# A two-layer gated cross-attention block on one core: start-up loads, key/value units ahead of attention, and one tile moved ahead of a LayerNorm

## The chip, the cores and the metric

The kernel runs on one core of a Trainium2 chip. A core has five engines, each with its own queue of instructions carried out in order: PE (TensorE, matrix products and transposes), DVE (VectorE), ACT (ScalarE), POOL (GpSimd) and SP (SyncE, which here issues the DMAs). They meet only at semaphores. The metric is the time of one execution on the device, in microseconds (us).

## The reference, cut to what matters

```
x = x + tanh(g_xattn[0]) * experts(layernorm(x), token_ids, ctx)       # stage 1: ctx is keys and values of four experts
x = x + tanh(g_ffn[0])   * bitnet_ffn(layernorm(x), Wgate, Wup, Wdown) # stage 2: 8-bit tokens, ternary weights, Hadamard
x = x + tanh(g_xattn[1]) * attention(layernorm(x), ctx, Wq, Wk, Wv, Wo) # stage 3: 16 heads of 128, softmax
x = x + tanh(g_ffn[1])   * moe(layernorm(x))                            # stage 4: 32 small experts, top 8, and a shared one
```

x and ctx are 1024 tokens of 256 values. Experts: `silu(h @ Wg.T) * (h @ Wu.T) @ Wd.T` with Wg, Wu and Wd all equal to the expert's 256 rows of ctx; each token takes one expert. Attention needs keys `K = ctx @ Wk` and values `V = ctx @ Wv`, which depend on the input ctx and the weights alone.

## The kernel before

All products are float32, made of three products of rounded parts (high times low, low times high, high times high; lines 1557 to 1559). So every operand is split into a high part (made by ACT with a copy that rounds) and a low part (a subtraction on DVE or POOL).

The tokens are two groups (g = 0, 1) of four tiles of 128. PE's program is written out by hand: the expert scores (12 products of 512 columns per expert and group), the expert outputs (12 products for each of eight tiles, `y0` to `y7`), then a pipeline over eight tiles of the feed-forward part. Its stages are named by letters: Q (transposes of the quantised tokens), G and U (gate and up products), F (transposes of the inner values), H (Hadamard products), C (transposes of the quantised values), D (down products), N (transposes of the next LayerNorm), P (queries). After that 32 steps of attention, one per head and group, and at last stage 4.

Keys and values are made in 64 **units**. One unit is six products of 512 columns into one PSUM bank, an eviction by ACT, and one or two stores to HBM, from which attention reads them back. Four units share one 512 KB block of weights, which is loaded, split by ACT (`block_high`) and POOL (`block_low`), and lies in one of two slots. The table FILLS says where PE's program has units ahead of attention: before, 26 of them (`s0` and `s1` are at the very start, `y6` is behind tile 6 of the expert outputs, `u0` behind the up product of tile 0, and so on). The other 38 lie in the steps of attention, one or none in each half step (`m0`, `e0`, ...). PE waits before unit k until ACT has evicted unit k-2 (`kv_taken`), since the units ahead of attention use two banks in turn.

POOL's order in the feed-forward part: for each tile the four butterfly additions of the Hadamard step (`fly`, lines 632 to 638) once DVE has multiplied gate and up (`inner`, line 1362); behind tile 0 the low part of block 4, `block_low(4)`. DVE's order: additions of the expert outputs to x (line 1200), LayerNorm of group 0 and its quantisation, then group 1 likewise. `qtok` are quantised tokens, `am` the largest magnitude of each token.

## Time and profile before

| | us |
|---|---|
| median of three runs (lowest, highest) | 568.3 (567.09, 570.09) |
| the profiled execution, its own time | 568.33 |
| its span in the trace | 566.5 |
| PE busy | 537.0 (95%) |
| DVE busy | 389.8 (69%) |
| ACT busy | 350.9 (62%) |
| POOL busy | 320.5 (57%) |

The time of an execution has 1.8 us more than the span, in which the trace shows no instruction. PE's instructions overlap, so that the ends of its rows are modelled; the distance from start to start tells what one takes. The column for PE's clock tells what the throttle granted. "idle before" is how long an engine did nothing before an instruction, with the engine that ended it.

### The profile page before, as it was taken

Reading aid. Unit: us, or ns where it says so; the run is one execution under the profiler, and the core shown is the slowest. Engines: PE = TensorE matmul, PEld = TensorE weight load, DVE = VectorE, ACT = ScalarE, POOL = GpSimd, SP = SyncE. Lnnn points to the kernel's source line nnn. Section 1 sums busy time; section 2 is a strip of 40 time slices with the busy share of each in tenths; the row PEclk is TensorE's granted clock in tenths of the full one; section 3 lists DMA queues with packets and bytes.
Section 4 is the critical chain, followed back from the end, with each engine's and each line's share of the span. In section 5 each row is a group of like instructions: output and inputs, shape, how many; then the busy total and the mean of one; then the engine's idle time right before and its main releaser. Section 6 shows DMA issues by size and latency. Waiting matters only on the chain.

```text
span 566.5 us, 9626 instructions
## 1 busy us (share of the span) xinstructions
PE 537.0 (95%) x3240; PEld 462.2 (82%) x3240; DVE 389.8 (69%) x822; ACT 350.9 (62%) x723; POOL 320.5 (57%) x320
## 2 busy tenths in 40 slices
PE   3999998998999999999999999999999989999997
PEld 3877766777778988999999999989998878777786
DVE  4867988689956575656655576646665757878883
ACT  3651155666478676766757565745757665777882
POOL 2579137999348797655544424426698465762220
PEclk9999999999999999999999999989999998999999
DMA  8901136510057768677696768534354735356651
GB/s 278 357 23 46 47 111 185 189 38 1 20 185 226 222 186 261 218 247 224 217 289 191 244 206 229 188 98 163 115 189 149 241 125 174 112 146 189 217 178 39
DMA packets 66672, 95.78 MB, mean 169 GB/s; under 512 B 6336, under 2 KB 38848, under 8 KB 66624
## 3 DMA queue, kind: packets, MB, share of 16 engines
q1 hardware_dynamic: 66624, 95.17, 53.0%
q8 instruction: 27, 0.44, 0.3%
q14 instruction: 21, 0.17, 0.1%
HBM read 67.23 MB, written 27.92 MB: 168 GB/s over the span
## 4 chain that ended last, share of the span: by engine, by line
PE 69%; DVE 11%; POOL 6%; ACT 5%; issue 4%; DMA 3%; SPq 1%; DVEq 0%; POOLq 0%
PE ps L1557 20%; PE ps L1558 19%; PE ps L1559 19%; PE ps L1662 4%; PE ps L1767 2%; PE ps L1751 2%; DMA k_hl<-k_scratch 1%; DVE e_r L1472 1%; PE ps L1774 1%; DMA blk_raw<-in_w_blocks 1%; DVE qtok L1223 1%; ACT q2T L921 1%; PE ps L1780 1%; DMA cw_row<-cw_scratch 1%; DVE e_lo L1482 1%
## 5 line engine op out<-in xcount | busy, mean ns | idle before, releaser
L657 POOL TENSOR_TENSOR probs<-probs,rsum 128x512 f32<-128x512 f32 x64 | 66.4, 1041 | 60.5 <-DVE rsum L1252 60.4
L1247 DVE TENSOR_REDUCE nmax<-ps 128x2 f32<-128x512 f32 x64 | 44.0, 688 | 35.6 <-PE ps L1559 35.3
L959 ACT ACTIVATE probs<-ps,nmax 128x256 f32<-128x256 f32 x128 | 59.7, 481 | 1.6 <-DVE nmax L1247 1.4
L578 POOL TENSOR_TENSOR kv_w_lo<-blk_raw,kv_w_hi 128x1024 fp32r<-128x1024 f32 x16 | 38.9, 2431 | 37.2 <-ACT kv_w_hi L826 37.2
L1045 ACT ACTIVATE e_hi<-e_r 128x512 fp32r<-128x512 f32 x64 | 40.2, 629 | 30.4 <-DVE e_r L1472 29.6
L1472 DVE SCALAR_TENSOR_TENSOR e_r<-ps,cw_row 128x512 f32<-128x512 f32 x64 | 43.6, 684 | 12.8 <-PE ps L1559 10.3
L1238 DVE TENSOR_TENSOR pT_lo<-ps,pT_hi 128x512 fp32r<-128x512 f32 x64 | 43.7, 685 | 11.9 <-ACT pT_hi L965 11.4
L780 POOL TENSOR_TENSOR e_lo<-e_sq,e_hi 128x512 fp32r<-128x512 f32 x19 | 24.5, 1292 | 45.1 <-ACT e_sq L1051 42.6
L1243 DVE TENSOR_TENSOR oT_lo<-ps,oT_hi 128x512 fp32r<-128x512 f32 x32 | 22.1, 691 | 40.2 <-ACT oT_hi L969 40.2
L965 ACT ACTIVATE pT_hi<-ps 128x512 fp32r<-128x512 f32 x64 | 38.3, 600 | 15.9 <-PE ps L1662 15.8
L969 ACT ACTIVATE oT_hi<-ps 128x512 fp32r<-128x512 f32 x32 | 19.1, 597 | 40.8 <-PE ps L1559 40.8
L584 POOL TENSOR_TENSOR k_hl<-k_hl 128x512 fp32r<-128x512 f32 x18 | 23.8, 1322 | 32.1 <-ACT k_hl L894 32.1
L1662 PE MATMUL ps<-eye,probs 128*128 128x128 f32 x256 | 39.0, 275 | 1.6 <-DVE kv_out L1278 1.0
L837 ACT ACTIVATE kv_hi<-ps 128x512 fp32r<-128x512 f32 x38 | 22.9, 602 | 26.9 <-PE ps L1559 26.9
L1557 PE MATMUL ps<-pT_hi,v_hl 128*128 128x256 f32 x128 | 36.6, 286 | 1.1 <-DVE pT_lo L1238 0.5
L1557 PE MATMUL ps<-k_hl,qT_lo 128*128 128x256 f32 x128 | 37.3, 292 | 0.0
L1559 PE MATMUL ps<-k_hl,qT_hi 128*128 128x256 f32 x128 | 36.4, 285 | 0.0
L1558 PE MATMUL ps<-k_hl,qT_hi 128*128 128x256 f32 x128 | 36.3, 284 | 0.0
L1559 PE MATMUL ps<-wo_hi,oT_hi 128*128 128x256 f32 x128 | 36.2, 283 | 0.0
L1558 PE MATMUL ps<-wo_lo,oT_hi 128*128 128x256 f32 x128 | 36.2, 283 | 0.0
L1557 PE MATMUL ps<-wo_hi,oT_lo 128*128 128x256 f32 x128 | 36.2, 283 | 0.0
L1559 PE MATMUL ps<-pT_hi,v_hl 128*128 128x256 f32 x128 | 36.2, 282 | 0.0
(299 smaller groups left out, 1876.9 us busy)
## 6 DMA issues: line engine op xcount, KB each, us to landing
cw_row<-cw_scratch SPq DMA_DIRECT2D x64, 256.0 KB, 3.6
v_hl<-v_scratch SPq DMA_DIRECT2D x24, 512.0 KB, 3.6
blk_raw<-in_w_blocks SPq DMA_DIRECT2D x23, 512.0 KB, 4.4
k_scratch<-kv_out SPq DMA_DIRECT2D x32, 256.0 KB, 2.6
v_scratch<-kv_out SPq DMA_DIRECT2D x32, 256.0 KB, 3.2
k_hl<-k_scratch SPq DMA_DIRECT2D x14, 512.0 KB, 3.5
v_scratch<-kv_hi SPq DMA_DIRECT2D x24, 256.0 KB, 2.8
blk_raw<-in_w_tail SPq DMA_DIRECT2D x10, 512.0 KB, 4.6
```

Source lines behind the costliest of these rows:

```text
L578: nc.gpsimd.tensor_tensor(lo[:, :], blk_raw[j % 2][:, :], hi[:, :].bitcast(F32), ALU.subtract).then_inc(blk_done, 1)
L657: nc.gpsimd.tensor_tensor(probs[:, b, :, :], probs[:, b, :, :], rsum[:, b, :].unsqueeze(2).to_broadcast([P, 2, S]), ALU.mult).then_inc(pro ...
L959: last = nc.scalar.activation(probs[:, b, t, :], ps[:, S_BANK[b], t * S:(t + 1) * S], ACT.Exp, bias=nmax[:, b, t:t + 1], accum_out=esum[:, ...
L965: nc.scalar.activation(pT_hi[:, b, :, :].rearrange("p k q -> p (k q)"), ps[:, P_BANK[b], :], ACT.Copy).then_inc(p_hi_done, 1)
L1045: nc.scalar.activation(e_hi[i % 4][:, :], e_r[i % 2][:, :], ACT.Square).then_inc(e_hi_done, 1)
L1238: V.tensor_tensor(pT_lo[:, b, :, :].rearrange("p k q -> p (k q)"), ps[:, P_BANK[b], :], pT_hi[:, b, :, :].rearrange("p k q -> p (k q)").bi ...
L1247: V.tensor_reduce(nmax[:, b, :], ps[:, S_BANK[b], :].rearrange("p (t k) -> p t k", t=2), AX.X, ALU.max, negate=True).then_inc(max_done, 1)
L1472: V.scalar_tensor_tensor(e_r[i % 2][:, :], ps[:, UP_BANK[i % 4], :], 0.0, cw_row[i % 4][:, :], ALU.max, ALU.mult).then_inc(root_done, 1)
L1557: mm(dst, l_lo, r_hi, start=first, stop=False, **kw)
L1558: mm(dst, l_hi, r_lo, start=False, stop=False, **kw)
L1559: return mm(dst, l_hi, r_hi, start=False, stop=last, **kw)
L1662: last = nc.tensor.transpose(ps[:, P_BANK[b], k * S + t * P:k * S + (t + 1) * P], probs[:, b, t, k * P:(k + 1) * P], ident)
```

## The change

It has these parts:

- **Start.** The first block of key weights and the first half of ctx are loaded in four pieces (128, 256, 256 and 384 KB) and split in as many. Until they come PE does ten products of zeros that nothing reads. The four units of `s0` (before three) do their products as high-high, low-high, high-low, so that each waits only for what it needs. The two units of `s1` (before one) do four of their six products ahead of the transposes of the first LayerNorm and the other two behind them. Their context is split on DVE right behind the first LayerNorm.
- **POOL's start.** The token masks are made in halves and later; `block_low(1)` comes before the rounding of the ternary weights, not before the third of them. On ACT `block_high(1)` comes ahead of the first silu.
- **Expert outputs.** The first tile of outputs is added to x ahead of the low part of z of group 1. Q of group 0 transposes in two halves, each waiting for one bank.
- **Tile 0 of the feed-forward part.** DVE multiplies its inner values ahead of the LayerNorm of group 1. Those of tile 1 come ahead of the quantisation of group 1. The rounding of that quantisation goes from DVE to ACT (`second_tokens`), between the first and the second eviction of `u1`.
- **Units.** 28 of the 64 units lie ahead of attention: one more each in `s0`, `s1` and `d4` (behind D of tile 4), one less in `d6`. All later units are numbered two further, and the blocks follow in another order.

```diff
-        BLOCKS = [("K", 0), ("V", 0), ("K", 1), ("V", 1), ("K", 2), ("Q", 0), ("K", 3), ("O", 0), ("V", 2), ("Q", 1), ("V", 3),
-                  ("O", 1), ("V", 0), ("Q", 2), ("K", 1), ("O", 2), ("V", 1), ("Q", 3), ("K", 2), ("V", 2), ("O", 3),
+        BLOCKS = [("K", 0), ("V", 0), ("K", 1), ("V", 1), ("K", 2), ("Q", 0), ("K", 3), ("V", 2), ("O", 0), ("Q", 1), ("V", 3),
+                  ("V", 0), ("O", 1), ("K", 1), ("Q", 2), ("O", 2), ("V", 1), ("K", 2), ("Q", 3), ("V", 2), ("O", 3),
...
-        FILLS = {"s0": 3, "s1": 1, "a11": 1, "y2": 1, "y6": 4, "u0": 2, "g1": 1, "u1": 3, "f0": 3, "g2": 1, "f1": 2, "d4": 0, "d5": 1, "c6": 1, "d6": 2}
+        FILLS = {"s0": 4, "s1": 2, "a11": 1, "y2": 1, "y6": 4, "u0": 2, "g1": 1, "u1": 3, "f0": 3, "g2": 1, "f1": 2, "d4": 1, "d5": 1, "c6": 1, "d6": 1}
...
+            sp.dma_start(blk_raw[0][:, 0:D], w_blocks[0, 0, :, 0:D]).then_inc(ld_keys[0], 16)
+            for c in range(DC):
+                sp.dma_start(cT_raw[:, c, 0:GT], ctx_t[c * P:(c + 1) * P, 0:GT]).then_inc(ld_ctx[c], 16)
+            sp.dma_start(blk_raw[0][:, D:4 * D], w_blocks[0, 0, :, D:4 * D]).then_inc(ld_keys[1], 16)
             sp.dma_start(xr[:, 0:GN, :], x[0:GT, :].rearrange("(n p) d -> p n d", p=P)).then_inc(ld_x[0], 16)
             sp.dma_start(eye[:, :], ident_in).then_inc(ld_const, 16)
-            load_context(1)
+            sp.dma_start(cT_raw[:, :, GT:T], ctx_t[:, GT:T].rearrange("(c p) n -> p c n", p=P)).then_inc(ld_ctx[2], 16)
...
+                for k in FILL_AT["s0"][2 * i:2 * i + 2]:
+                    store_unit(k)
...
-                pool.wait_ge(blk_hi_done, j + 1)
+                pool.wait_ge(blk_hi_done, j)
...
-            pool.wait_ge(blk_hi_done, 1)
             for n in range(4):
                 s = slice(n * D, (n + 1) * D)
+                pool.wait_ge(first_keys_hi_done, 1 if n == 0 else 2)
                 nc.gpsimd.tensor_tensor(kv_w_lo[0][:, s], blk_raw[0][:, s], kv_w_hi[0][:, s].bitcast(F32), ALU.subtract)\
                     .then_inc(first_keys_done if n < 3 else blk_done, 1)
             pool.wait_ge(ld_ids, 32)
-            for e in range(1, NB):
-                nc.gpsimd.tensor_scalar(ge_row[:, e - 1, :], ids_row[:, :], float(e * TOK_PER_EXPERT), None, ALU.is_ge)\
-                    .then_inc(masks_ready, 1)
+            for g in range(NG):
+                s = slice(g * GT, (g + 1) * GT)
+                if g:
+                    pool.wait_ge(h_ready, NG)
+                else:
+                    pool.wait_ge(ctx_late_done, DC)
+                for e in range(1, NB):
+                    nc.gpsimd.tensor_scalar(ge_row[:, e - 1, s], ids_row[:, s], float(e * TOK_PER_EXPERT), None, ALU.is_ge)\
+                        .then_inc(masks_ready, 1)
+            block_low(1)
             for i in range(3):
-                if i == 2:
-                    block_low(1)
...
-            pool.wait_ge(scales_ready, 1)
             block_low(2)
             block_low(3)
...
-                elif n == 7:
-                    key_low(1)
 
             pool.wait_ge(h_ready, NG + 1)
             block_low(7)
+            key_low(1)
             block_low(8)
             block_low(9)
...
+            act.wait_ge(ld_keys[0], 16)
+            nc.scalar.activation(kv_w_hi[0][:, 0:D], blk_raw[0][:, 0:D], ACT.Copy).then_inc(first_keys_hi_done, 1)
+            for c in range(DC):
+                act.wait_ge(ld_ctx[c], 16)
+                context_high(c, 0)
+            act.wait_ge(ld_keys[1], 16)
+            nc.scalar.activation(kv_w_hi[0][:, D:4 * D], blk_raw[0][:, D:4 * D], ACT.Copy).then_inc(first_keys_hi_done, 1)
+            for k in FILL_AT["s0"]:
+                if k == 2:
+                    act.wait_ge(ld_ctx[2], 16)
+                    for c in range(DC):
+                        context_high(c, 1)
+                take_unit(k)
...
+            block_high(1)
             for g in range(NG):
                 if g:
                     first_expert(g)
                     take("a11")
-                    block_high(1)
                 act.wait_ge(a_taken, (NB - 1) * (g + 1))
                 nc.scalar.activation(a_silu[:, :, :], a_sel[:, g, :, :], ACT.Silu).then_inc(a_silu_done, 1)
                 act.wait_ge(z_ready, g + 1)
                 nc.scalar.activation(z_hi[:, g, :, :], a_sel[:, g, :, :], ACT.Copy).then_inc(z_hi_done, 1)
             take("y2")
+            block_high(2)
             take("y6")
-            block_high(2)
+            block_high(3)
...
+            def second_tokens():
+
+                take_unit(FILL_AT["u1"][0])
+                act.wait_ge(q1_scaled, 1)
+                act.wait_ge(q1T_filled, 1)
+                for n in range(GN, NT):
+                    last = nc.scalar.activation(qtok[:, n - GN, :], h[:, n, :], ACT.Copy, scale=am_r[:, n:n + 1], bias=ROUND)
+                last.then_inc(q1_rounded, 1)
+                for k in FILL_AT["u1"][1:]:
+                    take_unit(k)
...
-                    take("u" + str(i))
-                if i < 2:
-                    block_high(3 + i)
+                    if i == 1:
+                        second_tokens()
+                    else:
+                        take("u" + str(i))
+                if i == 1:
+                    block_high(4)
...
+                    take("d4")
...
+            V.memset(zeros.bitcast(F32), 0.0).then_inc(zeros_ready, 1)
+            for c in range(DC):
+                dve.wait_ge(ctx_hi_done, c + 1)
+                V.tensor_tensor(cT_lo[:, c, 0:GT], cT_raw[:, c, 0:GT], cT_hi[:, c, 0:GT].bitcast(F32), ALU.subtract).then_inc(ctx_done, 1)
             dve.wait_ge(ld_x[0], 16)
             norm(0).then_inc(h_ready, 1)
+            for c in range(DC):
+                dve.wait_ge(ctx_hi_done, DC + c + 1)
+                V.tensor_tensor(cT_lo[:, c, GT:T], cT_raw[:, c, GT:T], cT_hi[:, c, GT:T].bitcast(F32), ALU.subtract).then_inc(ctx_late_done, 1)
...
-            context_low(1)
...
+                V.tensor_tensor(a_sel[:, g, :, :], a_sel[:, g, :, :], a_silu[:, :, :], ALU.mult).then_inc(z_ready, 1)
+                if g:
+                    add_experts([0])
+                dve.wait_ge(z_hi_done, g + 1)
+                V.tensor_tensor(z_lo[:, g, :, :], a_sel[:, g, :, :], z_hi[:, g, :, :].bitcast(F32), ALU.subtract).then_inc(z_done, 1)
...
+            def token_scales(g):
 
                 s = slice(g * GN, (g + 1) * GN)
                 own(V.tensor_reduce(am[:, s], h[:, s, :], AX.X, ALU.max, apply_absolute_value=True))
-                own(V.tensor_scalar(am[:, s], am[:, s], Q_EPS, None, ALU.max))
-                own(V.reciprocal(am_r[:, s], am[:, s]))
-                own(V.tensor_scalar(am_r[:, s], am_r[:, s], 128.0, None, ALU.mult))
+                own(V.tensor_scalar(am_c[:, s], am[:, s], Q_EPS, 1.0 / 128.0, ALU.max, ALU.mult))
+                return V.reciprocal(am_r[:, s], am_c[:, s])
+
+            def quantise(g):
+
+                s = slice(g * GN, (g + 1) * GN)
                 if g:
-                    dve.wait_ge(q1T_filled, g)
-                for n in range(GN):
-                    last = V.tensor_scalar(qtok[:, n, :], h[:, g * GN + n, :], am_r[:, g * GN + n:g * GN + n + 1], ROUND,
-                                           ALU.mult, ALU.add)
-                own(last)
+                    dve.wait_ge(q1_rounded, 1)
+                else:
+                    own(token_scales(0))
+                    for n in range(GN):
+                        last = V.tensor_scalar(qtok[:, n, :], h[:, n, :], am_r[:, n:n + 1], ROUND, ALU.mult, ALU.add)
+                    own(last)
...
+            inner_values(0)
             dve.wait_ge(y0_taken, NT)
             own(norm(1, 2))
             for i in range(NT + 3):
                 if i == NT + 2:
                     query_low(0)
                     query_low(1)
-                if i < NT:
-
-                    b = pair_of["U", i]
-                    dve.wait_ge(silu_done, i + 1)
-                    dve.wait_ge(up_values_filled, i + 1)
-                    V.tensor_tensor(inner[:, i % 2, :], inner[:, i % 2, :], ps[:, b:b + 2, :].rearrange("p a n -> p (a n)"),
-                                    ALU.mult).then_inc(inner_done, 1)
-                if i == 0:
+                if 0 < i < NT:
+                    inner_values(i)
+                if i == 1:
+                    token_scales(1).then_inc(q1_scaled, 1)
                     quantise(1)
...
+            def first_keys_begin(k):
+
+                kind, quad, n, g, j = UNITS[k]
+                tokens = slice(g * GT, (g + 1) * GT)
+                pe.wait_ge(first_keys_hi_done, 1 if n == 0 else 2)
+                for c in range(DC):
+                    pe.wait_ge(ctx_hi_done, g * DC + c + 1)
+                    mm(ps[:, fill_bank(k), :], kv_w_hi[0][:, (n * DC + c) * P:(n * DC + c + 1) * P], cT_hi[:, c, tokens],
+                       start=(c == 0), stop=False)
+                if n == 3:
+                    pe.wait_ge(blk_done, 1)
+                else:
+                    pe.wait_ge(first_keys_done, n + 1)
+                for c in range(DC):
+                    mm(ps[:, fill_bank(k), :], kv_w_lo[0][:, (n * DC + c) * P:(n * DC + c + 1) * P], cT_hi[:, c, tokens],
+                       start=False, stop=False)
+
+            def first_keys_end(k):
+
+                kind, quad, n, g, j = UNITS[k]
+                for c in range(DC):
+                    pe.wait_ge(ctx_late_done if g else ctx_done, c + 1)
+                    last = mm(ps[:, fill_bank(k), :], kv_w_hi[0][:, (n * DC + c) * P:(n * DC + c + 1) * P],
+                              cT_lo[:, c, g * GT:(g + 1) * GT], start=False, stop=(c == DC - 1))
+                last.then_inc(kv_filled, 1)
...
+                    if k < 2 * GN:
+                        first_keys_begin(k)
+                        first_keys_end(k)
+                        continue
...
-                    for c in range(DC):
+                    chunks = range(DC) if n else [fill_bank(k) - b for k in FILL_AT["y6"][-2:]]
+                    for c in chunks:
+                        if n == 0:
+                            pe.wait_ge(kv_taken, FILL_AT["y6"][-2:][chunks.index(c)] + 1)
...
+            pe.wait_ge(zeros_ready, 1)
+            for _ in range(10):
+                mm(ps[:, 7, :], zeros[:, 0:P], zeros, start=True, stop=True)
             fill_units("s0")
+            for k in fills("s1"):
+                pe.wait_ge(kv_taken, k - 1)
+                first_keys_begin(k)
             pe.wait_ge(ld_const, 16)
             transpose_norm(0, 0, 6)
-            fill_units("s1")
+            for k in fills("s1"):
+                first_keys_end(k)
```

How the order moves on PE at the start: the last unit of `s0`, the transposes of the first LayerNorm (`ps<-eye,h`) and `s1`. Before:

```order
L1557 MATMUL ps<-cT_hi,kv_w_lo0 128x512
L1558 MATMUL ps<-cT_lo,kv_w_hi0 128x512
L1559 MATMUL ps<-cT_hi,kv_w_hi0 128x512
L1571 MATMUL ps<-eye,h 128x128 x8
L1557 MATMUL ps<-cT_hi,kv_w_lo0 128x512
L1558 MATMUL ps<-cT_lo,kv_w_hi0 128x512
L1559 MATMUL ps<-cT_hi,kv_w_hi0 128x512
L1557 MATMUL ps<-cT_hi,kv_w_lo0 128x512
L1558 MATMUL ps<-cT_lo,kv_w_hi0 128x512
L1559 MATMUL ps<-cT_hi,kv_w_hi0 128x512
L1557 MATMUL ps<-hT_hi,cT_lo 128x512
```

With the change:

```order
L1640 MATMUL ps<-cT_hi,kv_w_lo0 128x512 x2
L1648 MATMUL ps<-cT_lo,kv_w_hi0 128x512 x2
L1633 MATMUL ps<-cT_hi,kv_w_hi0 128x512 x2
L1640 MATMUL ps<-cT_hi,kv_w_lo0 128x512 x2
L1633 MATMUL ps<-cT_hi,kv_w_hi0 128x512 x2
L1640 MATMUL ps<-cT_hi,kv_w_lo0 128x512 x2
L1621 MATMUL ps<-eye,h 128x128 x8
L1648 MATMUL ps<-cT_lo,kv_w_hi0 128x512 x4
L1607 MATMUL ps<-hT_hi,cT_lo 128x512
L1608 MATMUL ps<-hT_lo,cT_hi 128x512
L1609 MATMUL ps<-hT_hi,cT_hi 128x512
```

The transposes now stand behind four whole units and the first eight products of two more, whose last four products follow them.

How it moves on ACT, from the silu of tile 1 (`inner<-ps,c_gate`) on. Before:

```order
L910 ACTIVATE inner<-ps,c_gate 128x1024
L835 ACTIVATE kv_out<-ps 128x512 x4
L826 ACTIVATE kv_w_hi<-blk_raw 128x1024
L925 ACTIVATE fT_hi<-ps 128x1024
L835 ACTIVATE kv_out<-ps 128x512 x3
L910 ACTIVATE inner<-ps,c_gate 128x1024
```

With the change:

```order
L947 ACTIVATE inner<-ps,c_gate 128x1024
L846 ACTIVATE kv_out<-ps 128x512 x2
L923 ACTIVATE qtok<-h,am_r 128x256 x4
L846 ACTIVATE kv_out<-ps 128x512 x2
L838 ACTIVATE kv_w_hi<-blk_raw 128x1024
L965 ACTIVATE fT_hi<-ps 128x1024
L846 ACTIVATE kv_out<-ps 128x512 x3
L947 ACTIVATE inner<-ps,c_gate 128x1024
```

Four steps that write `qtok` now stand between two pairs of evictions, and `kv_w_hi` of block 4 behind them.

How it moves on DVE, between the last expert outputs (`xr<-ps,tgm,xr`) and the LayerNorm of group 1. Before:

```order
L1200 SCALAR_TENSOR_TENSOR xr<-ps,tgm,xr 128x256 x3
L1083 BN_STATS st<-xr 128x6 x2
L1088 BN_AGGR mv<-st 128x2 x4
L1091 TENSOR_SCALAR ln_v<-mv 128x4
L1094 TENSOR_SCALAR ln_i<-ln_v 128x4
```

With the change:

```order
L1219 SCALAR_TENSOR_TENSOR xr<-ps,tgm,xr 128x256 x3
L1281 TENSOR_TENSOR inner<-inner,ps 128x1024
L1124 BN_STATS st<-xr 128x6 x2
L1129 BN_AGGR mv<-st 128x2 x4
L1132 TENSOR_SCALAR ln_v<-mv 128x4
```

The multiplication of the inner values of tile 0 now stands ahead of the statistics.

## Rows read from the trace of the kernel before

**Rows 1.** Busy time by stretch: us, each engine (instructions), PE clock share, DMA share, GB/s.

```profile
0.00:163.00 163.00, 144.85 (x793) 114.15 (x794) 126.97 (x286) 81.03 (x97) 98.69 (x74) 1.00 0.37 121
163.00:420.00 257.00, 254.71 (x1720) 232.86 (x1720) 160.65 (x337) 172.76 (x442) 149.12 (x151) 0.99 0.66 207
```

**Rows 2.** The longest wait of PE up to 163 us: in total, times, longest.

```profile
PE ps L1557 <- POOL kv_w_lo L595: 8.7, 1, 8.7
```

**Rows 3.** Timeline of the start: us, duration, engine, line, operation [idle before].

```profile
12.27 0.63 PE L1559 MATMUL ps<-cT_hi,kv_w_hi 128*128 128x512 f32 x1
12.69 0.63 PE L1557 MATMUL ps<-cT_hi,kv_w_lo 128*128 128x512 f32 x1
12.88 2.10 DVE L1113 TENSOR_SCALAR h<-xr,mv,ln_y 128x256 f32<-128x256 f32 x4
13.13 8.67 POOL L599 TENSOR_SCALAR ge_row<-ids_row 128x1024 int32<-128x1024 int32 x3 [2.49 <-DMA ids_col<-in_ids]
14.41 0.39 PE L1557 MATMUL ps<-cT_hi,kv_w_lo 128*128 128x512 f32 x1
14.64 0.39 PE L1558 MATMUL ps<-cT_lo,kv_w_hi 128*128 128x512 f32 x1
16.42 0.69 DVE L1143 TENSOR_TENSOR hT_lo<-ps,hT_hi 128x512 fp32r<-128x512 f32 x1 [0.78 <-ACT hT_hi L848]
17.95 1.22 DVE L1133 TENSOR_TENSOR cT_lo<-cT_raw,cT_hi 128x1024 fp32r<-128x1024 f32 x1
18.11 0.47 PE L1557 MATMUL ps<-hT_hi,cT_lo 128*128 128x512 f32 x1
```

**Rows 4.** Timeline of the expert choice, ACT and DVE.

```profile
32.86 2.10 DVE L1186 TENSOR_TENSOR a_sel<-a_sel,a_silu 128x1024 f32<-128x1024 f32 x1 [1.06 <-ACT a_silu L877]
35.96 1.01 ACT L859 ACTIVATE a_sel<-ps 128x1024 f32<-128x1024 f32 x1
37.45 0.60 ACT L835 ACTIVATE kv_out<-ps 128x512 f32<-128x512 f32 x1 [0.47 <-PE ps L1559]
```

**Rows 5.** Timeline, the two waits of PE in the expert outputs.

```profile
53.87 0.50 PE L1557 MATMUL ps<-cT_hi,z_lo 128*128 128x512 f32 x1 [1.07 <-DVE xr L1200]
71.48 1.09 PE L1742 MATMUL ps<-eye,qtok 128*128 128x128 f32 x8 [0.69 <-ACT kv_out L835]
```

**Rows 6.** Timeline of the first tiles of the feed-forward part, and a contended step at 143 us.

```profile
77.69 0.75 DVE L1083 BATCH_NORM_STATS2 st<-xr 128x6 f32<-128x256 f32 x2
79.10 0.17 DVE L1094 TENSOR_SCALAR ln_i<-ln_v 128x4 int32<-128x4 int32 x1
82.70 1.22 DVE L1362 TENSOR_TENSOR inner<-inner,ps 128x1024 f32<-128x1024 f32 x1
83.83 1.21 DVE L1216 TENSOR_REDUCE am<-h 128x4 f32<-128x1024 f32 x1
84.87 1.29 POOL L632 TENSOR_TENSOR fly<-inner 128x512 f32<-128x512 f32 x1
89.99 2.44 POOL L578 TENSOR_TENSOR kv_w_lo<-blk_raw,kv_w_hi 128x1024 fp32r<-128x1024 f32 x1
90.17 1.06 PE L1757 MATMUL ps<-eye,inner 128*128 128x128 f32 x8 [2.12 <-POOL inner L638]
100.52 1.06 PE L1757 MATMUL ps<-eye,inner 128*128 128x128 f32 x8 [0.20 <-POOL inner L638]
143.12 1.27 POOL L584 TENSOR_TENSOR k_hl<-k_hl 128x512 fp32r<-128x512 f32 x1
143.22 1.20 DVE L1094 TENSOR_SCALAR ln_i<-ln_v 128x4 int32<-128x4 int32 x1
```

**Rows 7.** Timeline of the last tiles of the feed-forward part.

```profile
140.84 0.47 DVE L1388 SCALAR_TENSOR_TENSOR xr<-ps,am,xr 128x256 f32<-128x256 f32 x1
141.02 0.47 PE L1767 MATMUL ps<-had,fT_lo 128*128 128x256 f32 x2 [1.17 <-issue]
148.52 0.47 PE L1767 MATMUL ps<-had,fT_lo 128*128 128x256 f32 x2 [1.02 <-ACT q L931]
```

More of the change, by code:

```diff
@@ L106, in flamingo_two_layer_kernel @@
         head_weights(1, early)
+        zeros = wq_hi[1][:, 0:512]
         region = ExitStack()
@@ L839, in _, with context_high @@
-            for g in range(NG):
-                s = slice(g * GT, (g + 1) * GT)
-                act.wait_ge(ld_ctx[g], 16)
-                nc.scalar.activation(cT_hi[:, :, s], cT_raw[:, :, s], ACT.Copy).then_inc(ctx_hi_done, 1)
-                if g == 0:
-                    block_high(0)
-            take("s0")
+                    take_unit(k)
+            def context_high(c, g):
+                nc.scalar.activation(cT_hi[:, c, g * GT:(g + 1) * GT], cT_raw[:, c, g * GT:(g + 1) * GT], ACT.Copy).then_inc(ctx_hi_done, 1)
```

131 lines of the change are left out of this document (63 added, 68 removed).

## The prediction, made before the changed kernel was run

> **What bounds the kernel now.** I read busy time by stretch first, to see where PE leaves time unused. From 163 to 420 us, the attention steps, PE is busy 254.7 of 257 us: there only less work for PE brings time. Up to 163 us it is busy 144.9, so 18 us are idle [rows 1]. The waits of PE say who ends them: 8.7 us are the start, until the first low parts of the keys are there [rows 2]; the rest is waits of about 1 to 2 us, which I looked up one by one in the timeline [rows 5 to 7]. Work that the change moves out of attention is worth its full length if it fits into such idle time, and nothing otherwise.
>
> One unit is six products of 512 columns. They start 0.43 us apart at 12.27 and 12.69 us, and 0.23 apart at 14.41 and 14.64 [rows 3], so a unit costs 6 x 0.233 = 1.4 us there, and 2.6 at the slow spacing. By columns over spacing these are the clock levels of 1.2 and 2.4 GHz; PE had issued products back to back for 4.4 us (8.7 to 13.1) before the faster one. The column for the granted clock reads 1.00 for the whole part up to 163 us [rows 1] and doesn't show this; the spacing does.
>
> **The change part by part.** Times are those of the profiled execution, 568.33 us (span 566.5 and 1.8 around it); the median of the three runs is 568.3, so the sum stands for it too.
>
> *Start: two more units.* Whether they are free depends on when the expert products run without a wait, at 18.11 us before [rows 3]. That is set by DVE, which makes the low parts of the transposes (the first at 16.42) just before. DVE's last step of the LayerNorm (12.88 to 14.98) takes 2.10 us beside POOL's masks; the masks now come later, and without them I expect 0.7 us less, 14.3. But 1.22 us of context splitting, which lay behind at 17.95, now stand ahead of the low parts. DVE was idle for 0.78 us there, waiting for ACT, and the splitting fills that [rows 3]: 18.1 - 0.7 + 1.2 - 0.8 = 17.8, and with a gap between five steps instead of four 18.1 again. PE's side has room: with loads in pieces real products can start by about 6 us (estimate: 1 MB came by 6.7, when ACT began on the last of it in the chain), four units at 1.4 take it to 11.9 and eight products to 13.8, ahead of the transposes at about 14.3. Even at the slow spacing until 10 us it gets there by 14.5, so the zeros matter little. Two units fewer remain in attention, where PE is full: -2 x 1.4 = **-2.8**. Bounds: -4.2 (free at 16.7) and 0 (free at 20.9).
>
> *ACT ahead of the first silu.* `block_high(1)` is a pass over 1024 columns, about 1.0 us like the copy at 35.96 [rows 4]. Behind it in ACT's queue stand silu, z and the copy of the first expert of group 1, which PE needs for its third expert. That copy ended at 36.97, and PE's unit before the third expert ended at about 37.4 (ACT took it at 37.45): 0.4 us of slack. 1.05 - 0.4 = **+0.7**. Bounds: 0, as the multiplication (2.10 us at 32.86, held by POOL) may now find a gap, and +1.7, if it is held for one more pass of POOL.
>
> *Expert outputs.* The wait of 1.07 at 53.87 is for the first tile's addition, which now uses DVE's idle time while ACT makes z: **-1.1** (-1.1 to 0). Q's wait of 0.69 at 71.48 [rows 5] is for the last bank; half of the transposes (0.45 us) now goes into it: **-0.4** (-0.7 to 0). The wait before `u0` stays, since that is PE's own last tile and its additions behind it.
>
> *First tiles of the feed-forward part.* This is the part that decides. Before, PE waits 2.12 us at 90.17 for tile 0's butterfly on POOL, and that waits for `inner` at 82.70, which stood behind the LayerNorm begun at 77.69. Now `inner` is first: 77.7 to 78.9, and POOL's four additions of 1.29 us run from 79.0 to 84.2. That wait is gone. What is late next: the LayerNorm now runs beside POOL. At 143.22 `ln_i`, 0.17 us when alone at 79.10, took 1.20, as long as POOL's addition at 143.12 beside it [rows 6]. So of its three short steps `ln_v` gets in at 80.4, `ln_i` at 81.7, `ln_y` at 83.1. Nine Newton steps at 0.195 (estimate from those 0.17 and the gap behind them) end at 84.9, `h` at 1.4 later (2.10 less the 0.7) at 86.3, `inner` of tile 1 (1.22) at 87.5, the maximum (1.21) at 88.7, two small steps at 89.2. Only then may ACT round: four passes over 256 columns at about 0.4 (estimate: 0.60 for 512, 1.01 for 1024 in rows 4), to 90.8. Behind them in ACT's queue stand the evictions of the last two units of `u1`, and PE needs the first of these, at 91.4, for `f0`. PE has done F of tile 0 by 88.7: it waits 2.7 us. The block for the third unit of `f0` is late too: ACT splits it from 92.0 to 93.1, POOL (2.44) to 95.5; PE would want it at 94.2: 1.3 us more. New waits 4.0, old ones 2.12 and 0.37 (from the end of H to F of tile 1 at 100.52): **+1.5**. Bounds: -2.5 if no new wait arises, +5.6 if all four steps of `h` are held for 1.0 us each as well.
>
> A page says more. By the Trainium skill, "SBUF — State Buffer", section "Who interferes with whom", a DVE step with both inputs in SBUF is also held by a POOL instruction that reads SBUF. The Newton steps are such, and by it the first of them would wait until POOL's last addition at 84.2 and all behind it come about 1.0 later, 567.4 in the sum below. No row here shows a Newton step beside an addition of POOL; the split of the context at 17.95, both inputs in SBUF, took 1.22 beside the masks [rows 3], which is no hold by a pass of POOL of 8.67 / 3 = 2.9 us. I keep 1.5.
>
> *Last tiles.* The unit `d4` waits for D of tile 4 to be added to x, which ended at 140.84 + 0.47 = 141.3, while PE's next product came at 141.02 after 1.17 idle. It pushes H of tile 6 by 1.4 + 0.3 = 1.7. The next wait, 1.02 at 148.52 [rows 7], is filled, and one unit less stands in `d6`. There the queries wait for the transposes of the LayerNorm, whose eviction stands in ACT's queue behind tile 7, which is 0.4 late: **+0.3** (-1.4 to +1.5).
>
> *Rest.* Two more heads get keys that must be split again on ACT and POOL; both are below 70% busy from 163 to 420 (172.8 and 149.1 of 257, rows 1), so 0 (to +0.5). Stores ahead of the weight loads: 0; if late they would hold ACT's first sums.
>
> Sum: -2.8 + 0.7 - 1.1 - 0.4 + 1.5 + 0.3 = -1.8, so 568.3 - 1.8 = **566.5 us**.
>
> **The rivals.**
> - *The tile moved ahead is a clear gain.* If the short LayerNorm steps slip in between POOL's additions, `q1_scaled` comes 2.3 us earlier (86.9); both new waits shrink to 0.4 and about 1.3, that is 1.7 against 2.5: -0.8 in place of +1.5, **564.2**. For it: steps over PSUM or of one input don't all lengthen. Against: 143.22.
> - *The two units are not free.* If `h` keeps its 2.10 us beside POOL's last key pieces (+0.7 against my sum) and x lands 1.5 us later behind four loads instead of two, the expert products run freely 2.2 us later, at 20.3: -0.6 in place of -2.8, **568.7**. For it: two more issues stand ahead of x on SP. Against it: the bytes ahead of x are the same.
> - *Slower: ACT's queue is held by the token scales.* Each us that DVE is later with `q1_scaled` than 89.2 delays `f0` by one. From 91.0 on the whole gain is gone; with `h` held in all four steps (+4.1) it is 93.3, and the time **570.6**. It is decided by whether POOL still adds when `h` starts at 84.9; by my account it ended at 84.2.
> - *The zeros don't raise the clock, and products with gaps stay at 0.43 us.* Then PE reaches the transposes at 6 + 28 x 0.43 = 18.0, not 14.3, but DVE has split meanwhile; the expert products are free at about 20.2: **568.6**.
>
> **How the numbers follow.** Forecast 0.47 (its own range 564.9 to 568.2), clear gain 0.21, units not free 0.15, slower 0.10, clock 0.07. A measurement of this kernel can tell about 0.5%, 2.8 us, from no change: below 565.5 is faster, above 571.1 slower. Faster: the second case nearly whole (0.19) and a third of the forecast (0.16), 0.35; slower: half of the slow case and tails of the others, 0.10; the same 0.55. The range goes from 562.9 (the clear gain with no hold on ACT, 0.7, and with noise like the 1.2 below the median of the three runs) to 570.4.
>
> **What would show it.** Expert products without a wait at 18 us with six units behind them, and 36 units in attention; a wait of nothing at the tile 3 output; the wait at tile 1's POOL addition gone, and in its place one before the first unit of `f0`, ended by ACT `kv_out`, and one before its third, ended by POOL `kv_w_lo`; `ln_i` and `ln_y` over 1 us long. I am wrong if PE does `f0` without a wait, or if it starts the expert products later than 20 us.

## The result, and the profile after

| | before | after |
|---|---|---|
| median of 20 runs each | 567.92 us | 565.66 us (563.25 to 569.04) |
| ratio, 95% interval | | 0.9957 [0.9946, 0.9968] |
| profiled execution, its span | 568.33, 566.5 | 563.25, 561.5 |
| granted clock of the profiled execution | 0.994 | 1.000 |

The change brings 2.4 us (1.8 to 3.1); 1.8 were forecast. Two executions at a low granted clock, one of before with 664.61 us and one of experiment 3 with 755.92, are in no ratio. The two profiled executions differ by more, 5.1 us, since they had different clocks. I therefore place the difference by landmarks of PE, instructions that both kernels have, instead of by the spans:

| first product of | before | after | difference | added in this part |
|---|---|---|---|---|
| expert products without a wait | 18.11 | 17.31 | -0.80 | -0.80, with two units more done |
| `u0` | 77.81 | 75.28 | -2.53 | -1.73 |
| Q of tile 1 (transposes) | 105.08 | 104.30 | -0.78 | +1.75 |
| queries of attention | 158.22 | 158.02 | -0.20 | +0.58 |
| last transposes of probs | 435.36 | 431.22 | -4.14 | -3.94, of which 1.56 is one stretch at the slow clock in before |

The 1.56 is read from the same two instructions in both traces, before first, then after: they are 4.90 us apart in before and 3.34 in after. Between them before's products of 512 columns start 0.43 us apart instead of 0.23.

```profile
374.92 0.36 PE L1557 MATMUL ps<-k_hl,qT_lo 128*128 128x256 f32 x1
379.82 0.60 PE L1662 MATMUL ps<-eye,probs 128*128 128x128 f32 x4
```

```profile
372.30 0.36 PE L1607 MATMUL ps<-k_hl,qT_lo 128*128 128x256 f32 x1
375.64 0.60 PE L1739 MATMUL ps<-eye,probs 128*128 128x128 f32 x4
```

Without it attention brings -2.38, and the landmarks together -2.58. A second such stretch, from 471 to 474 us in before, costs 1.53 more; without both the spans differ by 1.9 us instead of 5.0.

The busy time by stretch of after (as in [rows 1]): PE now idles 12 instead of 18 us up to 163.

```profile
0.00:163.00 163.00, 150.78 (x810) 118.34 (x817) 121.43 (x282) 84.19 (x106) 99.66 (x77) 1.00 0.38 124
163.00:420.00 257.00, 254.43 (x1739) 233.09 (x1738) 161.73 (x340) 175.18 (x450) 155.37 (x159) 1.00 0.66 203
```

Three of the waits of PE up to 163 us (total, times, longest). The 8.7 of [rows 2] are gone; the longest is new, and ended by ACT:

```profile
PE ps L1607 <- ACT kv_out L846: 3.1, 1, 3.1
PE ps L1607 <- DVE xr L1438: 1.6, 1, 1.6
PE ps L1607 <- POOL kv_w_lo L587: 0.8, 1, 0.8
```

The timeline of the start, answering [rows 3]. The ten products of zeros are the first row (the zeros lie in the place of `wq_hi`), the first pair of real products is at 5.87, and `h` takes 1.38 instead of 2.10:

```profile
1.44 4.64 PE L1863 MATMUL ps<-wq_hi 128*128 128x512 f32 x10 [1.44 <-DVE wq_hi L1171]
5.87 0.82 PE L1633 MATMUL ps<-cT_hi,kv_w_hi 128*128 128x512 f32 x2
12.49 1.38 DVE L1154 TENSOR_SCALAR h<-xr,mv,ln_y 128x256 f32<-128x256 f32 x4
15.66 0.68 DVE L1185 TENSOR_TENSOR hT_lo<-ps,hT_hi 128x512 fp32r<-128x512 f32 x1
17.31 0.50 PE L1607 MATMUL ps<-hT_hi,cT_lo 128*128 128x512 f32 x1
```

The timeline of the expert choice, answering [rows 4]. The multiplication took 1.23, not 2.10, so silu could come later and the copy at 35.28 still come earlier:

```profile
29.52 1.05 ACT L838 ACTIVATE kv_w_hi<-blk_raw 128x1024 fp32r<-128x1024 f32 x1
33.05 1.23 DVE L1249 TENSOR_TENSOR a_sel<-a_sel,a_silu 128x1024 f32<-128x1024 f32 x1 [2.00 <-ACT a_silu L902]
35.28 1.01 ACT L884 ACTIVATE a_sel<-ps 128x1024 f32<-128x1024 f32 x1
```

The timeline of the first tiles, DVE, POOL, ACT and PE, answering [rows 6]. Between `inner` of tile 0 and `inner` of tile 1 DVE's short steps are in one place 0.16 or 0.17 us long, in another 1.14 to 1.20; POOL adds from 76.35 to 81.49:

```profile
75.06 1.21 DVE L1281 TENSOR_TENSOR inner<-inner,ps 128x1024 f32<-128x1024 f32 x1
76.35 1.29 POOL L645 TENSOR_TENSOR fly<-inner 128x512 f32<-128x512 f32 x1 [3.57 <-DVE inner L1281]
77.70 1.20 DVE L1135 TENSOR_SCALAR ln_i<-ln_v 128x4 int32<-128x4 int32 x1
78.93 0.17 DVE L1136 TENSOR_SCALAR ln_y<-ln_i 128x4 int32<-128x4 int32 x1
79.14 1.14 DVE L1142 SCALAR_TENSOR_TENSOR ln_t<-ln_y 128x4 f32<-128x4 f32 x1
80.22 1.27 POOL L651 TENSOR_TENSOR inner<-fly 128x512 f32<-128x512 f32 x1
80.31 1.19 DVE L1143 TENSOR_TENSOR ln_t<-ln_t,ln_v 128x4 f32<-128x4 f32 x1
81.54 0.16 DVE L1144 SCALAR_TENSOR_TENSOR ln_y<-ln_t,ln_y 128x4 f32<-128x4 f32 x1
86.93 0.18 DVE L1260 RECIPROCAL am_r<-am_c 128x4 f32<-128x4 f32 x1
87.14 1.70 ACT L923 ACTIVATE qtok<-h,am_r 128x256 f32<-128x256 f32 x4 [3.71 <-DVE am_r L1260]
88.75 1.06 ACT L846 ACTIVATE kv_out<-ps 128x512 f32<-128x512 f32 x2
89.47 0.47 PE L1607 MATMUL ps<-kv_w_hi,cT_lo 128*128 128x512 f32 x1 [3.08 <-ACT kv_out L846]
93.27 0.50 PE L1607 MATMUL ps<-cT_hi,kv_w_lo 128*128 128x512 f32 x1 [0.84 <-POOL kv_w_lo L587]
```

The chain reads backwards: PE waits for ACT's eviction, that stood behind the rounding, that waited for `am_r`, and DVE was late with it.

The timeline of the last tiles, answering [rows 7]. PE waits 1.61 at `d4` instead of 1.17, and shortly before the queries:

```profile
140.84 0.47 PE L1607 MATMUL ps<-cT_hi,kv_w_lo 128*128 128x512 f32 x1 [1.61 <-DVE xr L1438]
142.51 0.17 DVE L1135 TENSOR_SCALAR ln_i<-ln_v 128x4 int32<-128x4 int32 x1
156.66 1.07 PE L1852 MATMUL ps<-eye,q 128*128 128x128 f32 x8 [0.54 <-DVE q L1442]
158.02 0.50 PE L1607 MATMUL ps<-hT_hi,wq_lo 128*128 128x512 f32 x1 [0.30 <-DVE hT_lo L1168]
```

### The profile page after: what moved, and what is told of

The parts are those of the page before. It is cut to its first block, busy times and chain, and to the rows that moved or that the text cites. A ratio compares the mean times of both kernels' runs of the same rounds, so it can differ in the third digit from the quotient of the medians.

```text
span 561.5 us, 9648 instructions
## 1 busy us (share of the span) xinstructions
PE 537.1 (96%) x3244; PEld 461.4 (82%) x3250; DVE 383.3 (68%) x815; ACT 353.6 (63%) x732; POOL 324.2 (58%) x325
## 4 chain that ended last, share of the span: by engine, by line
PE 68%; DVE 13%; POOL 5%; issue 5%; ACT 5%; DMA 2%; SPq 0%; DVEq 0%; POOLq 0%
PE ps L1607 19%; PE ps L1608 19%; PE ps L1609 19%; PE ps L1739 4%; DVE xr L1219 2%; PE ps L1845 2%; PE ps L1829 2%; DVE st L1124 1%; ACT q2T L961 1%; DMA xr<-in_x 1%; PE ps L1852 1%; DMA cw_row<-cw_scratch 1%; DVE e_r L1522 1%; DVE h L1154 1%; DVE e_lo L1532 1%
## 5 line engine op out<-in xcount | busy, mean ns | idle before, releaser
L1291 DVE TENSOR_TENSOR pT_lo<-ps,pT_hi 128x512 fp32r<-128x512 f32 x64 | 43.8, 686 | 12.3 <-ACT pT_hi L1006 11.8
L593 POOL TENSOR_TENSOR k_hl<-k_hl 128x512 fp32r<-128x512 f32 x20 | 26.4, 1321 | 37.0 <-ACT k_hl L931 37.0
L848 ACT ACTIVATE kv_hi<-ps 128x512 fp32r<-128x512 f32 x36 | 21.7, 603 | 25.3 <-PE ps L1609 25.3
L1608 PE MATMUL ps<-pT_lo,v_hl 128*128 128x256 f32 x128 | 36.2, 282 | 0.0
L1608 PE MATMUL ps<-k_hl,qT_hi 128*128 128x256 f32 x128 | 36.1, 282 | 0.0
```

Source lines behind the costliest of these rows:

```text
L1291: V.tensor_tensor(pT_lo[:, b, :, :].rearrange("p k q -> p (k q)"), ps[:, P_BANK[b], :], pT_hi[:, b, :, :].rearrange("p k q -> p (k q)").bi ...
L1608: mm(dst, l_hi, r_lo, start=False, stop=False, **kw)
```

## The experiments

Ratios are to the kernel before, from 4 to 12 runs of each experiment. A difference between two experiments is that of their ratios times 567.5 us, good to about 1.3 us. Finer statements rest on the traces, one of each kernel. They too scatter at the start, since x doesn't always land at the same time: the first step of the LayerNorm is at 8.25 in after and at 8.32 to 8.82 in the experiments, and what follows moves with it. So distances between landmarks are compared: the time from `u0` to Q of tile 1 is 27.27 in before and 29.02 in after, that from there to the queries 53.14 and 53.72.

**1. The evictions first.** On ACT:

```diff
-                take_unit(FILL_AT["u1"][0])
...
-                for k in FILL_AT["u1"][1:]:
-                    take_unit(k)
...
-                    if i == 1:
-                        second_tokens()
-                    else:
-                        take("u" + str(i))
+                    take("u" + str(i))
                 if i == 1:
                     block_high(4)
+                    second_tokens()
```

> The changed kernel, but in the first FFN tiles ACT evicts all three units of u1 and splits the high block before it waits for q1_scaled and rounds the tokens of tile 1. Theory 1 (ACT's queue is held by the token scales): the wait of 3.08 us of PE before f0, ended by ACT kv_out, goes; the rounding now ends later by the evictions, so what stands behind it (evictions of f0) may hold PE for about 1.3 us in f0. The first product of Q of tile 1 comes about 2 us earlier (102.3 instead of 104.3), the whole 1.5 to 3 us less than the changed kernel (565.66), 562.7 to 564.2. Theory 2 (the next limit is the chain on DVE and POOL behind it, so the wait only moves): the 3.08 goes and a wait of the same length stands before Q of tile 1 or at the butterfly of tile 1; Q of tile 1 within 0.5 us of 104.3, the whole unchanged within 0.5 us.

Measured 561.36 us, 0.9896 [0.9876, 0.9916]: 3.5 us less than the changed kernel. From `u0` to Q of tile 1 it takes 26.09, 2.9 less. The 3.08 is gone, and the wait foretold in `f0` is there:

```profile
90.72 0.47 PE L1602 MATMUL ps<-cT_hi,kv_w_lo 128*128 128x512 f32 x1 [1.24 <-ACT kv_out L846]
```

PE doesn't wait for the tokens of tile 1, although they are rounded later; the order of ACT's queue alone cost this time. Theory 2 is out.

**2. The rounding behind `f0`.**

As in 1, but ACT calls `second_tokens` behind the evictions of `f0`, and DVE's part moves behind the low parts of tile 0:

```diff
-                    quantise(1)
...
+                if i == 1:
+                    quantise(1)
```

> As the run with the evictions first, and besides ACT rounds the tokens of tile 1 only after the evictions of f0, and DVE's half of that rounding (quantise of tile 1) stands behind the transposes of tile 0. Theory 1 (ACT's queue): both waits of PE, 3.08 before f0 and 0.84 before its third unit, go: 3.9 us less at the start of P of tile 0 than the changed kernel, and about 561.8 in the whole. Theory 2 (the chain of tile 1's tokens, its rounding and transposes, is what PE is next waiting for): Q of tile 1 comes no earlier than 104.3 and PE waits in front of it, ended by the tokens' transposes; the whole within 0.5 us of the changed kernel.

Measured 560.71 us, 0.9887 [0.9866, 0.9907]: 4.0 less than the changed kernel; `u0` to Q of tile 1 is 25.36, 3.7 less. One wait of 0.50 remains, for POOL's block.

**3. No zeros.** The ten products and their memset are left out.

> The changed kernel without the ten products of zeros and the memset of their operand; nothing of the result is left out. Theory 1 (DVE's low parts set when the expert products run freely, PE has room): the first real products start 0.43 us apart for about 4 us from 5.9 on, PE comes to the transposes some 3 us later than with the zeros but still before the low parts, expert products free at 17.3 to 17.8 as before; the whole within 0.5 us of the changed kernel. Theory 2 (the fast start is what makes the room for two units): 28 products with part of them at 0.43 end at about 15.5, the transposes and the keys behind them come 1.5 to 2 us later, and the whole is 1.5 to 2 us more.

Measured 565.80 us, 0.9974 [0.9955, 0.9992]. The profiled execution is the one of 755.92 us, with the granted clock at 0.65 from about 10 us to the end, so its trace can't place the end of the start.

**4. The same again.**

> The kernel without the products of zeros once more, since the profiled execution of the first run ran at a granted clock of 0.656 from 10 us on and does not show the start, and its median (0.9974 of before against 0.9957 of the changed kernel) lies between the theories. Theory 1 (DVE sets the end of the start): expert products run freely at 17.3 to 17.8 us, as with the zeros. Theory 2 (the zeros make the room): at 18.5 to 19.3, and the ratio comes out 0.998 or more.

Measured 566.58 us, 0.9980 [0.9962, 0.9998]. Its timeline of PE: pairs of products 0.86 us apart until 12.2, then 0.46, and free expert products at 19.50, 2.2 us later than with the zeros:

```profile
6.48 0.80 PE L1632 MATMUL ps<-cT_hi,kv_w_hi 128*128 128x512 f32 x1 [0.87 <-ACT cT_hi L856]
11.34 1.06 PE L1632 MATMUL ps<-cT_hi,kv_w_hi 128*128 128x512 f32 x2
12.84 0.62 PE L1647 MATMUL ps<-cT_lo,kv_w_hi 128*128 128x512 f32 x2
19.50 0.50 PE L1606 MATMUL ps<-hT_hi,cT_lo 128*128 128x512 f32 x1
```

`u0` starts at 77.45, 2.2 later as well. By the trace the zeros are worth about 2 us, by the ratios of experiments 3 and 4 1.1 (0 to 2). Theory 2 holds by the trace; its ratio of 0.998 was met as well.

**5. Tile 0 back behind the LayerNorm.**

```diff
-            inner_values(0)
...
+            inner_values(0)
```

> The changed kernel with tile 0's multiplication by inner values back behind the LayerNorm of tile 1 on DVE, as in the kernel before. Theory 1 (my account, +1.5 predicted and 1.4 seen between u0 and Q of tile 1): the LayerNorm's short steps run unheld, the waits of 3.08 and 0.84 go, a wait of about 2 us for POOL's butterfly of tile 0 returns, and the whole is 1 to 1.5 us less than the changed kernel. Theory 2 (the move ahead was neutral or a gain): the whole is the same or up to 1.5 us more, and PE waits as long in other places.

Measured 561.13 us, 0.9893 [0.9874, 0.9912]: 3.6 less than the changed kernel, more than either theory gave. `u0` to Q of tile 1 is 26.20, 2.8 less: waits of 3.9 are gone, and PE waits once, 1.24 at 86.91, for the butterfly, where theory 1 had 2. Whether this together with experiment 1 or 2 brings more was not tested. This profiled execution lost 1.4 us to a slow stretch that begins with `d4` (windows of PE, with the granted clock behind the instructions):

```profile
136.00:140.00 4.00, 2.40 (x9) 0.77 0.00 0
140.00:144.00 4.00, 4.00 (x29) 0.80 0.17 66
```

**6. `d4` back.**

```diff
-        FILLS = {... "d4": 1, "d5": 1, "c6": 1, "d6": 1}
+        FILLS = {... "d4": 0, "d5": 1, "c6": 1, "d6": 2}
```

> The changed kernel with d4 holding no unit and d6 two, as in the kernel before; all else as changed. Theory 1: PE's wait of 1.61 us at 140.84 becomes the 1.17 that the kernel before had there, one of about 1.0 us returns in front of H of tile 7, and the waits of 0.54 and 0.30 in front of the last transposes and the queries go: first query product at 157.7, 0.3 us earlier than the 158.02 of the changed kernel. Theory 2 (the move is worth something, because the waits before the queries stay): 158.6 to 159.0.

Measured 562.83 us, 0.9920 [0.9901, 0.9940]: 2.1 less than the changed kernel. From Q of tile 1 to the queries it takes 52.14: 1.6 less than after, and 1.0 less than before. The wait of 1.0 at H of tile 7 did not return, against both theories; something else in the change had removed it. The wait of 1.17 returned:

```profile
141.15 0.47 PE L1845 MATMUL ps<-had,fT_lo 128*128 128x256 f32 x2 [1.17 <-issue]
```

**7. `key_low(1)` back as well**, on top of 6. POOL's pass for the keys of head 1 returns to where it was:

```diff
+                elif n == 7:
+                    key_low(1)
             pool.wait_ge(h_ready, NG + 1)
             block_low(7)
-            key_low(1)
```

> The changed kernel with d4 back in d6 (0.992 of before, no wait of PE at H of tile 7), and with POOL's key_low(1) back behind the additions of tile 7, where the kernel before had it. Theory 1 (that pass of POOL held ln_i for 1.20 us and so made the wait of 1.02 us before H of tile 7): ln_i takes about 1.2 us instead of 0.17, the wait of PE of about 1.0 us in front of H of tile 7 comes back, and the queries come 1.0 us later. Theory 2 (the wait of the kernel before came from something else in the order of ACT or DVE): ln_i is long, but there is no wait of PE at H of tile 7.

Measured 564.03 us, 0.9937 [0.9915, 0.9960], 1.0 more than 6. POOL, DVE and PE in its timeline:

```profile
144.68 1.27 POOL L593 TENSOR_TENSOR k_hl<-k_hl 128x512 fp32r<-128x512 f32 x1
144.78 1.20 DVE L1136 TENSOR_SCALAR ln_i<-ln_v 128x4 int32<-128x4 int32 x1
150.07 0.48 PE L1846 MATMUL ps<-had,fT_lo 128*128 128x256 f32 x2 [0.97 <-ACT q L972]
```

Theory 1 in each point: the pass holds `ln_i`, `am` is late, so ACT's `q` is, and PE waits. From Q of tile 1 to the queries it takes 53.19, as in before (53.14).

**8. Both**, 2 and 6 together.

> The evictions first and the rounding late (560.7 us median, 0.9887 of before) with, in addition, the unit d4 put back into d6, where the kernel before had it. Theory 1 (my sum for the last tiles, +0.3): the first product of the queries of the attention part comes 0.3 us earlier than 154.67, and the whole is 0.3 us less, 560.4. Theory 2 (d4 fills the wait of 1.17 at 141.02 of before, so taking it back loses that): 1 us or more later at the queries.

Measured 559.70 us, 0.9864 [0.9841, 0.9887]: the best version, 7.7 us under before and 5.3 under the changed kernel. `u0` to Q of tile 1 25.39, from there to the queries 52.12: the second is 1.6 less than in 2, as in 6. Theory 1 had the sign but 0.3 for 1.6.

**9. The high part of block 1 behind silu.** On ACT only:

```diff
-            block_high(1)
             for g in range(NG):
                 if g:
                     first_expert(g)
                     take("a11")
+                    block_high(1)
```

> The changed kernel with the split of the second block's high part on ACT back behind the take of the unit, so behind silu of the first tile. Theory 1 (what I saw in the changed kernel's trace: DVE's multiplication found a gap, 1.23 us instead of 2.10, so the pass of 1.05 us in front of silu costs PE nothing): u0 starts at 75.3 as in the changed kernel, and the whole is the same. Theory 2 (my prediction, +0.7): u0 starts 0.7 us earlier. Theory 3 (the multiplication is held again by POOL without the pass in front): nothing at PE either, but the multiplication takes 2.1 us instead of 1.23.

Measured 572.93 us, 1.0093 [1.0063, 1.0122], 7.7 more than the changed kernel; no theory had this. POOL's low part stands ahead of the rounding of the ternary weights and now waits for ACT. It starts at 38.63 instead of 30.66, the rounding behind it as much later, and PE waits 5.5 us in the expert outputs:

```profile
38.63 2.41 POOL L587 TENSOR_TENSOR kv_w_lo<-blk_raw,kv_w_hi 128x1024 fp32r<-128x1024 f32 x1 [11.36 <-ACT kv_w_hi L838]
```

```profile
71.33 1.09 PE L1820 MATMUL ps<-eye,qtok 128*128 128x128 f32 x8 [2.31 <-DVE qtok L1272]
75.64 0.80 PE L1607 MATMUL ps<-cT_hi,z_lo 128*128 128x512 f32 x1 [3.22 <-DVE xr L1219]
```

Behind these the clock fell: the windows of PE read 0.62 from 72 to 76 us and 0.52 from 76 to 80. From PE's first expert product to `u0` it takes 66.20 us, in the changed kernel 58.80; what the 7.4 have beyond the waits are mostly products at the slow spacing. All its runs have a granted clock of 0.984 to 0.990, those of the changed kernel 0.991 to 1.000.

**10. Both parts of block 1 back**, ACT's as in 9, POOL's between the second and the third rounding as in before.

```diff
-            block_low(1)
             for i in range(3):
+                if i == 2:
+                    block_low(1)
```

> The changed kernel with both halves of the split of block 1 where the kernel before had them: high behind silu on ACT, low behind two thirds of the rounding of the ternary weights on POOL. (With only the high part back, POOL's low part waited in front of the whole rounding, 8 us, and the run took 1.0093 of before.) Theory 1 (that loss was POOL's queue alone): no waits of 2.3 and 3.2 us at 71 and 76 us; u0 starts at 75.3 to 75.7 as in the changed kernel, so the move ahead of silu was worth nothing and cost nothing. Theory 2 (block 1 is wanted earlier by the two more units): a wait of PE before a11 or y2, u0 later than 76.5.

Measured 566.25 us, 0.9964 [0.9947, 0.9981], 0.4 more than the changed kernel. The waits of 9 are gone. `u0` comes 59.01 us after PE's first expert product (17.05), in the changed kernel 58.80 (16.48). So both moves together cost nothing and gave 0.2 us at most: seven traces of experiments that don't differ there have 58.76 to 58.80, but an eighth has 59.35. The multiplication took 2.12 us again, as in [rows 4]:

```profile
32.66 2.12 DVE L1250 TENSOR_TENSOR a_sel<-a_sel,a_silu 128x1024 f32<-128x1024 f32 x1 [1.04 <-ACT a_silu L903]
```

**11. The masks early.**

```diff
                 if g:
                     pool.wait_ge(h_ready, NG)
-                else:
-                    pool.wait_ge(ctx_late_done, DC)
```

> The changed kernel with POOL's masks of group 0 made as soon as the low parts of the first keys are done, as in the kernel before, instead of behind the split of the late context. Theory 1 (the masks are what made h take 2.10 us in the kernel before): h of group 0 takes 2.0 to 2.1 us instead of 1.38, the expert products run freely at 18.0 instead of 17.3, and all behind is 0.7 us later. Theory 2 (h was held by the low parts of the keys, or by nothing of POOL): h at 1.4, no change behind it.

Measured 565.78 us, 0.9962 [0.9942, 0.9982]. `h` takes 1.68, 0.30 more than in all traces with the late masks, and the expert products are free at 17.71. Of these 0.4 us 0.1 is x, which landed later: from the LayerNorm's first step on it takes 9.36 instead of 9.06. Both lie between the theories: the token ids land at 13.1, 0.5 us after the start of `h`, so POOL can hold only what is left of it:

```profile
12.60 1.68 DVE L1152 TENSOR_SCALAR h<-xr,mv,ln_y 128x256 f32<-128x256 f32 x4
13.16 5.23 POOL L612 TENSOR_SCALAR ge_row<-ids_row 128x512 int32<-128x512 int32 x3 [3.45 <-DMA ids_col<-in_ids]
```

**12. What a unit in attention is worth.** In the kernel before, in six units:

```diff
+                        if FRONT_UNITS + 12 <= k < FRONT_UNITS + 18:
+                            if c == 0:
+                                last = mm(ps[:, fill_bank(k), :], lhs[0], rhs[0], start=True, stop=True)
+                            continue
```

> The kernel before, with five of the six products left out in six units of attention (30 products of 512 columns; their keys and values are wrong by that). It measures what a unit taken out of attention is worth, without the start being changed. Theory 1 (PE alone bounds the attention steps): 30 x 0.233 = 7.0 us less than the kernel before, ratio 0.9877. Theory 2 (other engines are close behind PE, as the 2.5 instead of 2.8 us between the first query product and the last transposes of probs hint): 10% or more of it is lost, 6.3 us or less, ratio 0.989 or more. Theory 3 (one of them is the bound in these steps): under 3.5 us, 0.994 or more.

Measured 562.37 us, 0.9900 [0.9877, 0.9922], 5.7 less. Between the first and the last transposes of probs it takes 259.44 us; before took 265.84, 264.28 without the slow stretch. So 4.8 of 7.0 arrive, theory 2. Of the missing 2.2 1.5 are waits of PE from 170 to 270 us, where before has 0.3 in the same row:

```profile
PE ps L1557 <- DVE kv_out L1278: 1.8, 2, 0.9
```

## Why the prediction came out as it did

The sum was -1.8, the runs gave -2.4 and the landmarks -2.58. The mechanism and the decisive place were right. That the whole came so near is partly luck: the parts up to `u0` and in attention came out 1.3 better than the sum, the two parts behind `u0` 0.5 worse.

- *Two more units, -2.8:* attention brings 2.38 by the landmarks, and the expert products were free at 17.31, not at the 18.1 of my account, 0.8 more: together 3.2. I had reckoned `h` to end at 14.3 (13.87), and 1.22 of splitting plus a gap between five steps behind it. The split ran in two steps inside 1.29. The masks decide a part: 0.3 us with the ids as late as they are (experiment 11).
- *"The zeros matter little"* was the false step. I let real products run from 6 us on at the slow spacing until 10. Without the zeros there is a wait of 0.87 before 6.48, and the slow spacing lasts until 12.2 (experiment 4). The count was wrong too: four units and four products each of two more are 32 products, not 28. With 32 even my slow spacing until 10 gives 15.3, not 14.5. With 32 the last rival's 18.0 would be 19.8. Nor had PE room: even with the zeros its products follow each other without a wait from 9.02 to the transposes at 14.13, while `h` ended at 13.87. The zeros carry about 2 of the 3.2 us.
- *ACT ahead of silu, +0.7:* nothing, my lower bound. Coming 0.4 us later than in experiment 10 (33.05 against 32.66), the multiplication took 1.23 and not 2.1; by experiment 10 both moves of block 1 gained 0.2 us at most. What I had not priced is the other half: with POOL's low part moved ahead, ACT's move is what keeps POOL's queue running, worth 7.7 us (experiment 9).
- *Expert outputs, -1.5:* from the free expert products to `u0` it is -1.73, where this term and the one before gave -0.8. The wait of 1.07 is gone and 0.25 is left of 0.69.
- *First tiles, +1.5:* +1.75. Both new waits are where I put them, 3.08 for 2.7 and 0.84 for 1.3; experiments 1, 2 and 5 give them back. I had `ln_v`, `ln_i` and `ln_y` each held for one addition. In fact `ln_i` and the first two Newton steps were held, three short steps all the same, but the Newton steps ended 7.6 us behind the start of `u0` (82.88), in my account 7.1 (84.9). By the Trainium skill, "SBUF — State Buffer", section "Who interferes with whom", a DVE step with both inputs in SBUF is held by a POOL instruction that reads SBUF. The trace agrees beside additions: 1.14 and 1.19 there, 0.16 behind them. So the rule was right on which Newton steps are held, and I should have followed it, but not for its price: `am_r` was ready 11.8 us behind the start of `u0`, against 11.4 in my account and 1.0 more by the rule, since `ln_v` (0.28) and `ln_y` were hardly held. `ln_y` began at 78.93, 0.02 before POOL's next addition. Other rows go beyond that sentence. `ln_i` has one input and was held for 1.20, and in the kernel before two one-input steps on `am` and `am_r`, 0.17 long for group 0 (66.23, 66.65), took 1.10 and 1.00 beside additions (85.08, 86.43). Beside POOL's masks, from 20.56 to 21.54 us in before, Newton steps took 0.16 as if alone.
- *Last tiles, +0.3:* +0.58, but from two terms that I had wrong. The unit in `d4` costs 1.6 (experiments 6 and 8), since it waits 1.61 for the addition to x and then pushes tile 6 by its full length; I let it fill the 1.02 at 148.52. That wait was gone anyway: the change moves `key_low(1)` off the LayerNorm, worth 1.0 (experiment 7). The row at 143.12 stood in my own [rows 6], as the price of a hold; I didn't ask where its instruction goes.
- *Attention's rest, 0:* of the 2.8 us of two units 0.4 did not arrive, inside my bound of +0.5. With six units emptied 2.2 of 7.0 are lost, most of it in waits for DVE's `kv_out` (experiment 12).

Of the rivals, the clear gain had the wrong reason too: the short steps did not slip in. The gain of 5.3 that was to be had lay in ACT's queue and in `d4`. The slow rival did not come since POOL had stopped at 81.49, before `h`.

## What to carry to other kernels

An instruction that waits in an engine's queue holds the work behind it, whoever needs that: put evictions that PE wants ahead of a pass whose input comes late, and move the two halves of a split on two engines together. When a row serves as a price for contention, also follow the instruction in that row through the change. Filling a wait with a unit pays only if the unit itself is ready at the start of the wait.
